# Two gated blocks of attention and experts: keys and values of all batches made during the routing, and the chunks of a turn laid out anew

## What is computed

```
x = x + tanh(g_xattn[0]) * A0(ctx, layernorm(x))      # similarity of 4 heads, top 76 of 256 kept, mixed with layernorm(x)
x = x + tanh(g_ffn[0])   * F0(layernorm(x))           # 64 experts, top 8 per token, 256 -> 128 -> 256
x = x + tanh(g_xattn[1]) * A1(layernorm(x), ctx)      # 16 heads, causal; k, v = ctx @ Wkv.T
x = x + tanh(g_ffn[1])   * F1(layernorm(x))           # 8 experts, top 2, and a shared expert of two chunks

k, v = split(ctx @ Wkv_expand.T)                      # (256, 256) each, per batch
out = softmax(causal(q_h k_h^T / 4)) v_h              # 16 heads of 16
```

## Time and profile before

| | us |
|---|---|
| median of 3 runs | 613.92 (612.71 to 614.38) |
| the profiled execution | 607.06 |
| its span, first to last instruction | 605.3 |
| experts, 147 to 279 us of the span | 132.0 |
| turn 0, 310 to 382 | 72.0 |
| turn 1, 382 to 449.5 | 67.5 |
| turn 2, 449.5 to 516 | 66.5 |

### The profile page before, as it was taken

The page is one execution under the profiler, slowest core; times in us unless marked ns, Lnnn a source line. Parts: engine busy times, 40 slices in busy tenths (PEclk is TensorE's granted clock), DMA queues, the critical chain, the costliest instruction groups (busy, mean ns, idle before and its releaser), DMA issues.

```text
span 605.3 us, 9222 instructions
## 1 busy us (share of the span) xinstructions
PE 425.7 (70%) x2738; PEld 355.7 (59%) x2738; DVE 346.5 (57%) x1050; ACT 184.0 (30%) x377; POOL 146.3 (24%) x154
## 2 busy tenths in 40 slices
PE   5065553302999999997136637899699978999686
PEld 3043342202998889885025425787488856887586
DVE  2978875396344444443367803487547883681554
ACT  3212210100333333343611412525252342517231
POOL 1306675673000000002775370001710000000000
PEclk9976565555999999997557756999779996999899
DMA  7996222266699999993332130000310000000000
GB/s 272 427 410 264 88 96 79 78 238 211 209 301 322 324 312 326 377 396 128 100 91 67 38 104 0 1 2 16 100 44 0 2 0 0 18 2 2 2 17 18
DMA packets 36693, 82.96 MB, mean 137 GB/s; under 512 B 6000, under 2 KB 16048, under 8 KB 34864
## 3 DMA queue, kind: packets, MB, share of 16 engines
q1 hardware_dynamic: 22800, 55.83, 26.3%
q0 software_dynamic: 6144, 16.79, 8.6%
q10 hardware_dynamic: 7712, 9.90, 4.6%
HBM read 50.44 MB, written 31.92 MB: 136 GB/s over the span
## 4 chain that ended last, share of the span: by engine, by line
PE 52%; DVE 15%; issue 12%; ACT 7%; POOL 6%; another core or an unknown queue 4%; DMA 2%; SPq 1%; DVEq 0%; POOLq 0%; ACTq 0%
PE PS L555 11%; PE PS L565 7%; POOL slots_in L432 5%; PE PS L644 4%; PE PS L618 4%; PE PS L542 3%; PE PS L764 2%; PE PS L657 2%; PE PS L712 2%; PE PS L659 2%; PE PS L658 2%; DVE TH L1312 2%; DVE WORK L1049 2%; DVE TOP L1045 2%
## 5 line engine op out<-in xcount | busy, mean ns | idle before, releaser
L442 POOL DMA_INDIRECT GB<-slots_out,IDXG x64 | 68.4, 1069 | 214.9 <-SPq L365 139.7
L555 PE MATMUL PS<-XTE,WR 128*128 128x128 f32 (+2 forms) x512 | 79.7, 299 | 0.0
L432 POOL DMA_INDIRECT slots_in<-XNA,IDX x64 | 64.9, 1014 | 36.8 <-issue 27.6
L555 PEld LDWEIGHTS PS<-XTE,WR 128*128 128x128 f32 x512 | 70.2, 193 | 0.6 <-ACT XTE L854 0.4
L1234 DVE TENSOR_TENSOR HE<-SGE,PS 128x128 f32<-128x128 f32 (+2 forms) x64 | 20.0, 312 | 62.9 <-ACT SGE L863 60.0
L565 PE MATMUL PS<-WR,HE 128*80 128x256 f32 (+2 forms) x198 | 53.6, 381 | 0.3 <-DVE HE L1234 0.3
L657 PE MATMUL PS<-XH,WGH 128*128 128x256 f32 x160 | 49.7, 311 | 0.3 <-DVE XL L1430 0.3
L854 ACT COPY XTE<-PS 128x256 f32<-128x256 f32 (+2 forms) x64 | 26.3, 410 | 74.5 <-PE PS L542 70.6
L644 PE MATMUL PS<-WD,XW 128*128 128x256 f32 x160 | 41.8, 384 | 7.0 <-DVE XW L1319 3.5
L542 PE MATMUL PS<-CF,XE 80*128 80x80 f32 (+2 forms) x198 | 28.3, 256 | 25.7 <-DMA XE<-slots_in 25.7
L658 PE MATMUL PS<-XL,WGH 128*128 128x256 f32 x160 | 45.3, 283 | 0.0
(11 more groups left out here) (226 smaller groups left out, 843.2 us busy)
## 6 DMA issues: line engine op xcount, KB each, us to landing
WR<-in_wexp SPq DMA_DIRECT2D x64, 384.0 KB, 5.0
slots_in<-GB SPq DMA_DIRECT2D x12, 1024.0 KB, 18.7
XE<-slots_in SPq DMA_DIRECT2D x24, 160.0 KB, 4.5
slots_out<-OE ACTq DMA_DIRECT2D x24, 160.0 KB, 4.3
XE<-slots_in SPq DMA_DIRECT2D x29, 128.0 KB, 5.2
slots_out<-OE ACTq DMA_DIRECT2D x29, 128.0 KB, 5.1
WGU<-in_wgu SPq DMA_DIRECT2D x1, 2560.0 KB
XE<-slots_in SPq DMA_DIRECT2D x11, 192.0 KB, 4.0
```

What stands on the lines that cost most here:

```text
L432: pool.indirect_dma_start(out=xs, out_offset=bass.IndirectOffsetOnAxis(ap=IDX[:, t, j:j + 1], axis=0), in_=XNA[:, t, :], in_offset=None, b ...
L442: pool.indirect_dma_start(out=GB[:, t % BT, j, :], out_offset=None, in_=ys, in_offset=bass.IndirectOffsetOnAxis(ap=IDXG[:, t, j:j + 1], ax ...
L555: last = mm(psGE[place % 2][:, a, 0:cap(place)], W13[:, k, a, :], XTE[:, place % 2, k, 0:cap(place)], start=(k == 0), stop=(k == KC - 1))
```

## The change

Keys and values of all four batches are made during the routing, on PE and ACT, straight from CT. The spread keys are stored to a new tensor in HBM by two pairs of units at a time in KST, the values from VA. The low parts of the keys now come from PE (the product again, minus the high part by a negated identity) and not from DVE. SP loads keys and values back into KS and VA for each turn, once the last average of the turn before is done. POOL's copies to CTB are gone, and the weights WK, WV and SPREADB are loaded ahead of X. In a turn `fill(0)` to `fill(2)` each stand one step later, three chunks instead of two stand among the units, and of chunks 7 to 9 the rows (`up`) and the down product (`sum_down`) stand apart, in the tail. The experts wait for the store of the spread keys, since the memory of KP, SPREADK and KST is given to their buffers.

```diff
@@ names, SP @@
+            for dst, src in ((WK1[:, :, :], wk1), (WV1[:, :], wv1), (SPREADB[:, :, :, :], spread)):
+                sp.dma_start(dst, src).then_inc(S["loaded_kv"], 16)
             sp.dma_start(X[:, :, :], x.rearrange("(t p) d -> p t d", p=P)).then_inc(S["loaded_x"], 16)
...
             sp.wait_ge(S["scattered"], 16 * TT * TOP0)
+            sp.wait_ge(S["ks_kept"], 16 * B)
...
+            def keys_values(b):
+                sp.dma_start(KS[:, :, :].rearrange("p g n -> p (g n)").bitcast(F32), kst[ds(b * P, P), :]).then_inc(S["ks_in"], 16)
+                sp.dma_start(VA[:, :, :, :].rearrange("p t h c -> p (t h c)"), vst[ds(b * P, P), :]).then_inc(S["va_in"], 16)
+
+            def next_keys_values(b):
+
+                sp.wait_ge(S["e_av"], b * HG)
+                keys_values(b)
...
+            keys_values(0)
             maxima_rows(0)
-            with sp.Fori(0, B - 1) as f:
+            next_keys_values(1)
+            with sp.Fori(0, B - 2) as f:
                 maxima_rows(f + 1)
+                next_keys_values(f + 2)
                 store(f)
+            maxima_rows(B - 1)
+            store(B - 2)
             store(B - 1)
@@ PE, routing @@
+            def keys(b):
+                pe.wait_ge(S["qk_copied"], min(b + 2, B))
+                pe.wait_ge(S["sim_copied"], min(b + 2, B))
+                pe.wait_ge(S["ks_set"], b * 4)
+                for m in range(KC):
+                    last = mm(psKc[:, m, :], WK1[:, m, :], CT[:, b * N:(b + 1) * N], start=True, stop=True)
+                last.then_inc(S["k_done"], 1)
+                for t in range(BT):
+                    last = mm(psV[:, t, :], CT[:, b * N + t * P:b * N + (t + 1) * P], WV1[:, :], start=True, stop=True)
+                last.then_inc(S["v_done"], 1)
+
+            def keys_rest(b):
+                pe.wait_ge(S["k_high"], b + 1)
+                pe.wait_ge(S["va_set"], b + 1)
+                for m in range(KC):
+                    mm(psKl[:, m, :], WK1[:, m, :], CT[:, b * N:(b + 1) * N], start=True, stop=False)
+                    last = mm(psKl[:, m, :], NEG[:, :], KP[:, 0, m, :], start=False, stop=True)
+                last.then_inc(S["k_rest"], 1)
...
             scores(0)
             scores(1)
+            pe.wait_ge(S["loaded_kv"], 48)
+            pe.wait_ge(S["spread_set"], 2)
+            keys(0)
+            keys_rest(0)
+            spread_keys(0, 0)
             pe.wait_ge(S["loaded_gate0"], 48)
-            for b in range(B):
-                mix(b)
-                logits(b)
-                ranks(b)
-                if b + 2 < B:
-                    scores(b + 2)
+            mix(0)
+            spread_keys(0, 2)
+            logits(0)
+            ranks(0)
+            pe.wait_ge(S["ks_set"], 4)
+            scores(2)
+            keys(1)
+            mix(1)
+            keys_rest(1)
+            spread_keys(1, 0)
+            logits(1)
...
             last.then_inc(S["counted"], 1)
+            spread_keys(2, 2)
+            keys(3)
+            keys_rest(3)
             pe.wait_ge(S["order_set"], 1)
             mm(psOrder, numbersb[0:E0, :], OH[0:E0, :], start=True, stop=True)
             mm(psPlace, onesb[0:E0, :], DG[0:E0, :], start=True, stop=True).then_inc(S["order_done"], 1)
+            spread_keys(3, 0)
+            spread_keys(3, 2)
+            pe.wait_ge(S["ks_set"], 4 * B)
@@ PE, a turn @@
-                fill(0)
...
                 last.then_inc(S["e_flip"], 1)
-                fill(1)
+                fill(0)
...
                 last.then_inc(S["e_q"], 1)
+                fill(1)
...
+                pe.wait_ge(S["ks_in"], b * 16 + 16)
                 for u in range(UNITS):
...
-                    if u in (2, 5):
-                        fill(4 + u // 3)
+                    if u in (1, 3, 5):
+                        fill(3 + u // 2)
...
                 fill(6)
                 flip_maxima(b, 1)
-                fill(7)
...
                 average(HG - 1)
-                fill(8)
+                up(7)
...
                 last.then_inc(S["e_ot"], 1)
-                if ahead:
-                    keys(b + 1)
+                sum_down(6)
...
-                if ahead:
-                    pe.wait_ge(S["e_x3"], b + 1)
-                    values(b + 1)
-                    spread_keys(b + 1)
-                    pe.wait_ge(S["e_va"], b + 2)
-                fill(9)
+                up(8)
+                sum_down(7)
+                up(9)
                 pe.wait_ge(S["e_xn3"], b + 1)
...
-                if f is not None:
-                    down(f, NF - 1)
+                sum_down(8)
...
                 last.then_inc(S["e_gate"], 1)
+                sum_down(NF - 1)
```

209 lines of the change are left out of this document (126 added, 83 removed).

## The result

| | median us (range), 7 runs each |
|---|---|
| before | 613.92 (610.49 to 614.53) |
| changed | 616.74 (613.61 to 619.55) |
| ratio | 1.0066, 95% interval 1.0036 to 1.0096 |

The account below looks back on a forecast made before the run. PE work was taken to bound the turns from turn 1 on, a serial chain up to POOL's scatters the routing. Turns -13.5, routing +4, behind the last batch +2: -7.5, giving 606.4 us; 8-in-10 range 597 to 614.

Parts of the forecast that it names:

- The turns: Four attention turns together: -13.5 us, bounds -5 and -19; turns 0 to 3: -0.5, -3.5, -6 and -3.5.
- the place of chunk 7: Turns 2 and 3: chunk 7 no longer ahead of the heads on PE nor the combining on DVE, 2.3 us saved.
- the missing values and spreading: Turn 2's tail: without them on PE, the transposes follow the norm directly, 3.5 us sooner.
- the second rival: Tails: DVE's norm sets the end, so turns give only -6 and routing costs +6: 614 us, chance 0.10.
- The clock behind a thin tail: Start of turn 1: PE idles in turn 0's tail, so early work runs at the low clock, +2.5 us, up to +4.5.
- The whole 4.5 us: Start of turn 1: by the skill's clock-gate rule alone all 4.5 us would be paid, leaving turn 1 at -1.5.
- The routing chain: Routing: added keys and values on PE and ACT delay the first mix and its followers, +4 us, bounds -4 and +11.
- the later batches: Last three batches of the routing: no further delay, 0 us, bounds -4 and +5.7.
- behind the last batch: +2, at most +6: Between routing and experts: order 6.3 us later, token weights +1.2, weights' loads sharing DMA queues; +2 us, bounds 0 and +6.
- The first rival: Routing and order: low clock in all four batches, +11 there and +6 behind, outweighs the turns: 617 us, chance 0.13.
- The unnamed waits: ACT's unexplained waits in turn 0 move with its program: shrink, 596 us, chance 0.15; grow, 616 us, chance 0.05.
- The loads of keys and values: Loads for each turn: hidden with 20 us to spare, cost 0; rival that turns wait for late keys, chance 0.02.

Follow-up runs that it names:

- groups 2 and 3: The changed kernel unchanged, run again beside the kernel before on first-kind chips: 617.80 us (ratio 1.0123), then 616.00 us (1.0069).
- the layout alone: Kernel before with the chunks placed as in the change, keys and values left in the tails: 570.56 us (0.9734) on the second kind, 601.89 us (0.9853) on the first.
- group 3: Runs on one first-kind chip: kernel before 612.41 us, changed kernel 616.00 us, the layout alone 601.89 us, chunk 7 moved whole behind the heads 618.51 us.
- groups 1 and 5: Second-kind runs compared here: the layout alone, 570.56 us (0.9734), and the changed kernel unchanged, 579.59 us (0.9859).
- the order first: Also k3_order_first: changed kernel with the two products of the experts' order ahead of the last batch's keys on PE: 574.09 us, ratio 0.9792 to before.
- group 1: Second-kind runs of four kernels with parts or variants of the change, 570.56 to 592.44 us, against the kernel before at 587.59 us.
- group 5: Second-kind runs: the changed kernel unchanged, 579.59 us against 588.26 (0.9859), and the kernel before with POOL's gathers held, 663.26 us.
- the two runs meant to test that: Kernel before, with POOL's gathers for the next batch held until the turn's heads are copied: 664.38 us and 663.26 us, one run each.
- k3_again: Repeat of the changed kernel with the order's products ahead of the last batch's keys, second kind again: 573.33 us, ratio 0.9774 to before.
- k4_mix_first: Changed kernel with the order's products first and the first batch's mix ahead of its keys on PE: 578.86 us, ratio 0.9849 to before.
- k8_no_last: Changed kernel with the order's products first and the last batch's keys and values left out: 572.86 us, one run.

## Why the prediction was wrong

Profiled executions, first kind: three of before and three of the changed kernel (the result's, groups 2 and 3), and the layout alone beside them:

| us | before | changed | layout alone |
|---|---|---|---|
| experts' first product | 147.0, 147.9, 147.3 | 162.9, 167.2, 165.2 | 147.7 |
| from there to turn 0 | 163.7, 164.1, 164.7 | 163.7, 162.8, 163.8 | 163.3 |
| turn 0 | 70.8, 74.0, 74.0 | 72.5, 73.2, 74.3 | 74.0 |
| turn 1 | 68.2, 69.3, 70.5 | 68.5, 68.4, 67.3 | 68.2 |
| turn 2 | 66.4, 64.7, 64.7 | 59.5, 57.4, 59.3 | 61.6 |
| turn 3 | 59.4, 59.4, 59.4 | 55.1, 54.4, 55.2 | 56.6 |
| last chunks | 29.8, 29.7, 29.9 | 30.3, 31.4, 30.3 | 30.3 |

By means, the experts begin 17.7 us later, the turns with the last chunks take 11.0 us less (the turns alone 11.9) and the part between 0.7 less: some +6, against measured ratios that are worth 4 to 7.5 us.

- **The turns: nearly right in size, in part wrong in cause.** -13.5 was forecast, -11.9 came. Turns 2 and 3 gained 6.5 and 4.5 us by these executions (6 and 3.5 forecast), turn 1 some 1.3 (3.5), turn 0 nothing. For turn 2 I gave 2.3 us to the place of chunk 7 and 3.5 to the missing values and spreading. Moving a whole chunk 7 alone gave 2.5 there, but by keeping the clock up in the tail and not by heads that start sooner: those came only 1.8 us sooner, as the 2.3 read from the earlier trace rows has a flip of 0.38 in it, and the tail took that back. The layout alone gains 3.1 in turn 2 and the missing keys 2.3 more (61.6 against 59.3, both on the chip of group 3). In turn 3 the place of chunk 7, to which I gave 2.3 of 3.5, gives 0, and the layout 2.8: that is the halves, which I had not priced by themselves. Why turn 3 of the changed kernel is shorter still (55.2 against 56.6), though it has no keys in either, stays open. From the first flip to the end the missing keys, in the new layout, are worth 290.7 - 286.4 = 4.3 us on the first kind (group 3), and on the second 263.5 - 263.2 = 0.3 by the changed kernel (groups 1 and 5) or 263.5 - 261.2 = 2.3 by the one with the order first (group 1).

Why so little shows in the tails of turn 2 on the second kind, first the layout alone, then the order first (no keys there):

```profile
472.67 0.66 PE L768 MATMUL PS<-CF,X 128*128 128x128 f32 x4 [1.12 <-DVE X L1424]
474.00 1.99 PE L773 MATMUL PS<-WO,X 128*128 128x256 f32 x8 [0.68 <-ACT X L967]
...
479.27 2.18 PE L618 MATMUL PS<-KP,SPREAD 128*128 128x256 f32 x16
...
482.70 0.60 PE L787 MATMUL PS<-CF,EQ 128*128 128x128 f32 x4
```

```profile
474.75 0.66 PE L832 MATMUL PS<-CF,X 128*128 128x128 f32 x4 [2.36 <-DVE X L1506]
476.08 3.10 PE L837 MATMUL PS<-WO,X 128*128 128x256 f32 x8 [0.67 <-ACT X L1059]
...
484.12 0.66 PE L846 MATMUL PS<-CF,EQ 128*128 128x128 f32 x4 [0.74 <-DVE EQ L1129]
```

With the keys PE waits 1.12 us for the heads and the projection takes 1.99; without them it waits 2.36, drops to the lower clock, and the projection takes 3.10. From the projection's end to the transposes of the norm it is 6.7 us with keys and 4.9 without, and the 4.9 are DVE's. This is the reason of the second rival ("the tail belongs to DVE"), to which I gave 0.10. It holds for the keys on the second kind; its sum (-6 over the turns) does not, and it left out the halves.

- **The clock behind a thin tail: right in kind.** Turn 1 began at 0.50 in the result's trace, as forecast. By the traces of the second kind it cost 1.1 to 1.4 us at the turn's start, not 2.5. The whole 4.5 us of the Trainium skill's rule, as I worked it out ("TensorE: Matmul & The Clock Gate", Part 1, the HAM clock gate), did not come; its direction did. But the thin tail also slows its own products, as the 3.10 above shows, and that I had not counted: with the order first turn 1 lasts 61.5 us, with the layout alone 58.7 (second kind, one chip).
- **The routing chain: too small.** +4, at most +11, was forecast for the last scatter; 6.75 came. The first copy of X1 was at 40.2 as worked out, and the first scatter at 51.6. I took 0 for the later batches, and there the changed kernel lost 2.9 us at the second, which then stayed.
- **The step that failed is "behind the last batch: +2, at most +6".** I added up the order's delay (6.3 us behind the counts; 4.9 came), but charged it only to DVE's token weights. The counts themselves were 9.2 us late, which I had left at +4. With 7.3 us more of SyncE's reads, which I could not have read from before, the weights' loads left 21.4 us late, and SyncE had only 13 us to spare. They came onto the last scatters and the slots, together with the last store of the keys: 3.85 and 5.23 us by the chain's rows. I had named that meeting in a clause and given it no price of its own. This is 9 us where I took 2; in the two other traces, where SyncE issues the slots later than the scatters allow, it is more (experts 19.2 and 18.0 us late against the kernel before on the same chip, with the last scatter 5.7 and 6.7 late). Putting the order's products ahead of `keys(3)` takes 4.0 us of it back on the second kind (experts at 147.4 instead of 151.4, on different chips) and 8.9 on the first (158.3 instead of 167.2, one chip).
- **The first rival ("the routing chain eats it", 0.13) came true by its own condition**, routing and order together above 15 us, and its 617 us is what was measured. Its split was another: +11 in the chain and +6 behind it, where the result's trace has 6.75 and 9.1. Nor is its low clock in all four batches there: the keys of the last batch took 1.10 us, not 2.07. So that its number fits is in part luck.
- **The unnamed waits** neither vanished nor moved with the instructions as the rival had it. They hang on the chip: the same program has 45.6 us of them in the result and none in group 5. By the rule of the Trainium skill ("Runtime: NRT & Kernel Launch", instruction fetch mechanics) they would be blocks fetched late and would be the program's; the trace of the second kind, with the same program, doesn't agree. What they are stays open. All lie in stretches in which POOL's indirect transfers run beside PE and ACT, or within some 1 us of them; the two runs meant to test that were on chips without such waits.
- The loads of keys and values never made a turn wait, as said.

## What to carry to other kernels

Work without dependencies is not free in a phase that looks idle: add up the whole chain of one unit with its handovers at the clock of that phase (here 13.6 us a batch), and look at what each product it is put ahead of lets go; here two products of 0.24 us each released 3 MB of loads. Where a tail is bound by another engine's norm, taking PE's work out mostly moves the wait and lowers the clock; splitting what remains into halves, so that no product waits for a result behind that norm, paid (2.8 us in turn 3). One long wait can cost more than its length: broken up, the same tail kept the high clock and was 2.5 us shorter. And measure the parts of a change alone: the layout by itself is faster (0.985 and 0.973), the keys by themselves slower (1.011, on the second kind alone).

## What was not expected of the hardware

- Two kinds of chip: the kernel before takes 611 to 614 us on one and 584 to 588 on the other, and the change is 1.007 to 1.012 on the first and 0.986 on the second. A ratio of a per cent has to be taken on both.
- SyncE's reads of ORD get slower while a store of keys or values (1 or 0.5 MB) is under way: mostly 0.52 to 0.88 us instead of 0.26 to 0.28 (k3_order_first, k3_again, k4_mix_first, k8_no_last).
- On the first kind many of SyncE's register instructions took 0.70 us, most of which took 0.15 or less before, for 9 us and more, in every trace of a kernel with keys in the routing (from the order to the first issue 12.5, 13.5, 13.3 and 7.7 us) and in none without. Its cause is open.
- The same program's turn differs from one execution to the next by the clock at its start: in three traces of the changed kernel on the first kind turn 1's first head begins 29.4, 30.1 and 28.7 us into the turn.
